# A hybrid retention, mixture-of-experts and attention kernel: where the expert weights are staged, and which engine works out the normalizations' factors

## What is computed

```python
x = x + retention(layernorm(x))   # 2 layers, 16 heads of 8, FFN 512, norms with gain and bias
x = x + moe(layernorm(x))         # 8 experts, the 2 best per token, silu(x w1) * (x w3) w2, F = 512
x = x + attention(layernorm(x))   # 16 heads of 8, causal softmax
x = x + moe(layernorm(x))         # the same weights
```

## Time and profile before

| | us |
|---|---|
| median of 3 runs (lowest, highest) | 889.42 (888.31, 891.47) |
| the profiled execution | 889.34 |
| its span | 887.3 |
| busy: TensorE, VectorE, ScalarE, GpSimd | 654.9, 609.1, 354.8, 294.6 |
| share of the chain that ended last: PE, DVE, "issue" | 55%, 16%, 10% |

### The profile page before, as it was taken

The page is one execution under the profiler, slowest core; times in us unless marked ns, Lnnn a source line. Parts: engine busy times, 40 slices in busy tenths (PEclk is TensorE's granted clock), DMA queues, the critical chain, the costliest instruction groups (busy, mean ns, idle before and its releaser), DMA issues.

```text
span 887.3 us, 19344 instructions
## 1 busy us (share of the span) xinstructions
PE 654.9 (74%) x6492; PEld 453.9 (51%) x6492; DVE 609.1 (69%) x1789; ACT 354.8 (40%) x605; POOL 294.6 (33%) x602
## 2 busy tenths in 40 slices
PE   2758998667868520999935788898898982499990
PEld 1434654435536420999933234444444442399990
DVE  2687876554686883688855677678678735387874
ACT  3204555453533420444414045555564561244440
POOL 1113344141433575355530201110512222355551
PEclk9788999987998855899976589999999995699995
DMA  9995211121100031556533512221312000265554
GB/s 229 193 184 120 96 49 48 48 66 31 49 19 2 3 81 46 146 165 171 167 120 101 130 30 56 76 57 46 101 40 67 15 14 18 81 171 152 167 146 148
DMA packets 102265, 81.00 MB, mean 91 GB/s; under 512 B 8380, under 2 KB 92412, under 8 KB 101980
## 3 DMA queue, kind: packets, MB, share of 16 engines
q1 hardware_dynamic: 96568, 68.35, 31.9%
q0 software_dynamic: 4544, 9.38, 3.1%
q10 hardware_dynamic: 1056, 2.04, 0.6%
HBM read 54.56 MB, written 23.20 MB: 88 GB/s over the span
## 4 chain that ended last, share of the span: by engine, by line
PE 55%; DVE 16%; issue 10%; DMA 6%; POOL 6%; ACT 4%; SPq 2%; ACTq 0%; DVEq 0%; POOLq 0%
PE PC L1999 8%; PE PA L1989 5%; PE PB L1989 5%; DVE rmax L1374 4%; POOL rows_dram L775 4%; PE PC L1905 4%; PE P L2077 4%; PE PA L2037 3%; PE PA L1883 3%; PE PA L2035 3%; PE P L1934 3%; PE P L1925 2%; PE P L1808 2%; DMA ffn_w<-in_w 2%; PE PC L2060 2%
## 5 line engine op out<-in xcount | busy, mean ns | idle before, releaser
L1374 DVE TENSOR_REDUCE rmax<-PA 128x1 f32<-128x512 f32 (+3 forms) x256 | 120.0, 489 | 50.1 <-PE PA L2037 43.3
L787 POOL DMA_INDIRECT outs_dram<-va,ids x78 | 81.2, 1041 | 94.4 <-DVE va L1313 89.9
L1999 PE MATMUL PC<-ffn_w,pm 128*128 128x128 f32 x624 | 87.0, 283 | 3.2 <-DMA ffn_w<-in_w 3.1
L775 POOL DMA_INDIRECT rows_dram<-va,idx x64 | 63.2, 988 | 77.9 <-DVE va L1242 59.1
L2037 PE MATMUL PA<-kst,qst 96*128 96x512 bf16 (+3 forms) x256 | 83.7, 332 | 0.0
L2035 PE MATMUL PA<-mqb,idb 128*128 128x128 bf16 x256 | 60.3, 237 | 24.7 <-DVE rmax L1374 17.4
L1999 PEld LDWEIGHTS PC<-ffn_w,pm 128*128 128x128 f32 x624 | 75.8, 192 | 4.6 <-DMA ffn_w<-in_w 3.9
L1641 ACT ACTIVATE kv_b<-P 128x256 f16<-128x256 f16 x78 | 29.9, 383 | 116.2 <-PE P L1978 116.2
L1303 DVE SCALAR_TENSOR_TENSOR pm<-PB,invb,decay 128x512 f32<-128x512 f32 x78 | 58.5, 750 | 19.5 <-ACT decay L1649 12.8
L2035 PEld LDWEIGHTS PA<-mqb,idb 128*128 128x128 bf16 x256 | 25.3, 99 | 86.9 <-DVE rmax L1374 47.6
L1989 PE MATMUL PA<-kv_b,pm 128*128 128x128 f16 x936 | 66.9, 223 | 0.0
(11 more groups left out here) (239 smaller groups left out, 1472.7 us busy)
## 6 DMA issues: line engine op xcount, KB each, us to landing
ffn_w<-in_w SPq DMA_DIRECT2D x78, 256.0 KB
rows_dram<-wall SPq DMA_DIRECT2D x1, 8385.0 KB, 54.0
X<-in_w SPq DMA_DIRECT2D x32, 256.0 KB, 2.9
proj_w<-rows_dram SPq DMA_DIRECT2D x78, 65.0 KB, 2.0
qst<-parts_dram SPq DMA_DIRECT2D x48, 96.0 KB
kst<-parts_dram SPq DMA_DIRECT2D x48, 96.0 KB
parts_dram<-qkp SPq DMA_DIRECT2D x16, 256.0 KB, 2.7
R<-outs_dram SPq DMA_DIRECT2D x4, 512.0 KB, 3.8
```

The source lines that it names most:

```text
L775: nc.gpsimd.indirect_dma_start(out=rows_dram, out_offset=bass.IndirectOffsetOnAxis(ap=idx[:, t, r:r + 1], axis=0), in_=xrow[:, t, :], in_o ...
L787: nc.gpsimd.indirect_dma_start(out=outs_dram, out_offset=bass.IndirectOffsetOnAxis(ap=ids[:, k % YB:k % YB + 1], axis=0), in_=ysb[:, k % Y ...
L1374: nc.vector.tensor_reduce(rmax[:, i, h % HG:h % HG + 1], PA[:, n % 2, 0:(i + 1) * P], AX_X, ALU.max).then_inc(pair_sb[n % 2], 1)
L1999: ins = mm(PC[:, k % 2, 0:D], eT[:, k % 2, f, :], w2b[k % WB2][:, f, :], start=f == 0, stop=f == FB - 1)
```

## The change

- **Weights.** Eight staging buffers, one per expert, are laid over the first buffers of `qst` and `kst`; each expert is loaded once, right behind the other inputs. In the place of the maximum of absolute values on VectorE comes the sum of absolute values on ScalarE (`weight_sum`, two in each of steps 4 to 7). The scales are made in step 9, high halves in steps 10 to 17, low halves in steps 12 to 19. The pad write follows the sums.
- **X.** x stays in X and is not loaded again. `add_shift` follows in step 3 of units 2 to 5.
- **Factors.** `mean_factors` on VectorE takes the place of GpSimd's `norm_factors` at 12 places: in step 1 of units 1 to 7, in step 0 of units 3 to 6, and for (LNM1, 0). `leave(0)` moves from step 30 to 29. ScalarE normalizes (LNM1, 0) a step earlier, and the router's first turn and product move ahead in TensorE's and ScalarE's streams.
- **Constant rows.** They are made by GpSimd after the blocks and filled by SyncE (four fills of 384 KB, then bo) behind the third w2 load of the first expert stage.
- Some buffers are doubled for this (`xrow_`, `parts_`, `below_`, `oneb_`, `cnt_`), by reuse of others.

```diff
+SUMS_AT, SCALE_AT, HIGH_AT, LOW_AT = 4, 9, 10, 12
-        stage = tuple(X[:, 8 * b:8 * b + 8, :].rearrange("p t n -> p (t n)") for b in range(2))
+        raw = tuple(stack[:, 0, :].bitcast(F32) for stack in (qst, kst))
+        stage = tuple(raw[2 * e // E][:, e % (E // 2) * 2 * F:(e % (E // 2) + 1) * 2 * F] for e in range(E))
+        all_sums = wall32[:, 0:2 * F]
...
@@ SyncE @@
-            sp.wait_ge(filled, 2)
-            for stack, fill in ((qst, zeros), (kst, ones)):
-                sp.dma_start(stack[KQ:KS, 0, :].rearrange("r (h n) -> r h n", h=H),
-                             fill.unsqueeze(1).to_broadcast([KS - KQ, H, L])).then_inc(stack_fill, 16)
...
+            for e in range(E):
+                sp.dma_start(stage[e][:, 0:F], a_w1[e]).then_inc(stage_in[e], 16)
+                sp.dma_start(stage[e][:, F:2 * F], a_w3[e]).then_inc(stage_in[e], 16)
...
                     w2_load(n, expert[n])
+                    if (m, n) == (0, 2):
+                        stack_constants()
+                        sp.dma_start(bo[:, :], a_bo.partition_broadcast(P)).then_inc(in_att, 16)
...
+            def stack_constants():
+                sp.wait_ge(filled, 3)
+                for b in range(2):
+                    for stack, fill in ((qst, zeros), (kst, ones)):
+                        sp.dma_start(stack[KQ:KS, b, :].rearrange("r (h n) -> r h n", h=H),
+                                     fill.unsqueeze(1).to_broadcast([KS - KQ, H, L])).then_inc(stack_fill, 16)
+            largest_weights()
             pad_rows()
-            for e in range(2 * E):
-                expert_in(e)
-                if e == E - 1:
-                    largest_weights()
             sp.wait_ge(w_hi, E)
             sp.wait_ge(w_lo, E)
-            for s in range(SEQ):
-                sp.dma_start(X[:, TPS * s:TPS * s + TPS, :], x_t[:, TPS * s:TPS * s + TPS, :]).then_inc(x_back[s], 16)
             sp.wait_ge(sc_ps, 2 * LAST)
-            sp.dma_start(kst[KQ:KS, 1, :], kst[KQ:KS, 0, :]).then_inc(stack_again, 16)
             sp.wait_ge(stats_sb, STAT[(LNM1, SEQ - 1)] + 1)
-            sp.dma_start(qst[KQ:KS, 1, :], qst[KQ:KS, 0, :]).then_inc(stack_again, 16)
...
@@ GpSimd @@
-                    if n == UNITS - 1:
-                        add_shift(0)
                 if u == 1:
-                    if SEQ <= n + 1 < UNITS:
-                        norm_factors(STAT[ln_in(n + 1)])
...
-                if u == 2 and n >= 1:
-                    norm_factors(STAT[ln_up(n - 1)])
-            norm_factors(STAT[(LNM1, 0)])
+                if u == 3 and 2 <= n < SEQ + 2:
+                    add_shift(n - 2)
             add_ffn2(UNITS - 2)
-            add_shift(1)
...
+            constant_rows()
             norm_factors(STAT[(LNM1, 1)])
             add_ffn2(UNITS - 1)
-            add_shift(2)
-            add_shift(3)
             norm_factors(STAT[(LNM1, 2)])
...
@@ VectorE @@
+                    if TPS < t < LAST and u == 1:
+                        mean_factors(STAT[ln_up(n - 1)])
                     if u == 0 and 3 <= n < SEQ + 3:
                         row_sums(R, n - 3)
                         means(*ln_in(n + 1))
+                        mean_factors(STAT[ln_in(n + 1)])
...
-                    if E - 1 <= t < 2 * E - 1:
-                        largest_weight(t - E + 1)
-                    if t == 2 * E + 1:
+                    if t == SCALE_AT:
                         weight_scales()
-                    if 2 * E + 2 <= t < 3 * E + 2:
-                        low_weight(t - 2 * E - 2)
-                    if t == LAST - 2:
+                    if LOW_AT <= t < LOW_AT + E:
+                        low_weight(t - LOW_AT)
+                    if t == LAST - 3:
                         leave(0)
+                        mean_factors(STAT[(LNM1, 0)])
...
@@ ScalarE @@
+            def weight_sum(e):
+                act.wait_ge(stage_in[e], 32)
+                if e >= 2:
+                    act.wait_ge(w_max, e - 1)
+                nc.scalar.activation(wall32[:, (1 + e % 2) * 2 * F:(2 + e % 2) * 2 * F], stage[e], ACT.Abs,
+                                     accum_out=amax[:, e:e + 1]).then_inc(w_max, 1)
...
                 act.wait_ge(w_scaled, 1)
-                act.wait_ge(stage_in[e % 2], 32 * ((E + e) // 2 + 1))
...
                 def weights(t):
-                    if 2 * E + 2 <= t < 3 * E + 2:
-                        high_weight(t - 2 * E - 2)
+                    if SUMS_AT <= t < SUMS_AT + E // 2:
+                        weight_sum(2 * (t - SUMS_AT))
+                        weight_sum(2 * (t - SUMS_AT) + 1)
+                    if HIGH_AT <= t < HIGH_AT + E:
+                        high_weight(t - HIGH_AT)
...
+                    if n == UNITS - 1:
+                        normalize(LNM1, 0)
...
@@ TensorE @@
+                    if t == LAST:
+                        plain_turn(LNM1, 0)
+                    if t == LAST + 1:
+                        router(0, 0).then_inc(ring_ps, 1)
...
-                route(0, 0)
                 down(UNITS - 2)
```

More of the change, by code:

```diff
@@ L175, in ring_plan @@
         if n >= 2:
-            plan += [("up", n - 2, f) for f in range(FB)]
+            plan += [("up", n - 2, 0), ("up", n - 2, 1)]
+        if n == UNITS:
+            plan += [("turn", LNM1, 0)]
+        if n >= 2:
+            plan += [("up", n - 2, 2), ("up", n - 2, 3)]
+        if n == UNITS:
+            plan += [("router", 0, 0)]
         if n + 1 < UNITS:
             plan += front(n + 1)
-        if n == UNITS:
-            plan += route(0, 0)
         if n == UNITS + 1:
@@ L338, in mixer_kernel @@
         state = sb("state", [P, 2, D])
-        below = state[:, 0, 0:P // 2].bitcast(BF16)
-        oneb = state[:, 0, P // 2:P].bitcast(BF16)
+        xrow_ = (xrow0, xrow1)
+        parts_ = [x[:, :, 0:D].bitcast(F16).rearrange("p t (i n) -> p t i n", i=2) for x in xrow_]
+        below_ = [x[:, 0:P // 2].bitcast(BF16) for x in (bo, state[:, 0, :])]
+        oneb_ = [x[:, P // 2:P].bitcast(BF16) for x in (bo, state[:, 0, :])]
         idh = state[:, 1, 0:P // 2].bitcast(F16)
@@ L353, in mixer_kernel @@
         lge = sb("lge", [P, 2, TPS, E])
-        scratch = (late[:, 0:2 * TPS * E * E], R[:, 2 * TPS:3 * TPS, :].rearrange("p k n -> p (k n)"))
+        scratch = tuple(R[:, c * TPS:(c + 1) * TPS, :].rearrange("p k n -> p (k n)") for c in (0, 2))
         cgt_, cge_ = ([x[:, i * TPS * E * E:(i + 1) * TPS * E * E].rearrange("p (k a b) -> p k a b", k=TPS, a=E)
@@ L415, in mixer_kernel @@
         in_att = sem("in_att")
-        stage_in = (sem("stage_ina"), sem("stage_inb"))
+        stage_in = [sem(f"stage_in{e}") for e in range(E)]
         w_max = sem("w_max")
@@ L607, in largest_weights @@
                 sp.wait_ge(amax_out, 16)
[L608 removed]
+                sp.dma_start(all_sums.rearrange("p (r e) -> p r e", e=E),
                              amax_dram.partition_broadcast(P)).then_inc(amax_in, 16)
@@ L1621, in blocks @@
                         gelu(n - 2, 3)
+                    if n == UNITS:
+                        keep_logits(0, 0).then_inc(freed("router", 0, 0), 1)
                     weights(TPS * n + 1)
@@ L1837, in count @@
                 pe.wait_ge(routed, c + 1)
+                pe.wait_ge(att_const, 1)
                 w = TPS * E
-                mm(bank[:, 0:w], below, taken[:, c % 2, :], start=True, stop=False, skip_group_check=True)
+                mm(bank[:, 0:w], below_[m], taken[:, c % 2, :], start=True, stop=False, skip_group_check=True)
                 for k in range(1, TPS):
-                    mm(bank[:, k * E:w], oneb, taken[:, c % 2, 0:w - k * E], start=False, stop=k == TPS - 1,
+                    mm(bank[:, k * E:w], oneb_[m], taken[:, c % 2, 0:w - k * E], start=False, stop=k == TPS - 1,
                        skip_group_check=True)
                 for k in range(TPS):
-                    ins = mm(bank[:, w:w + E], oneb, taken[:, c % 2, k * E:(k + 1) * E], start=k == 0,
+                    ins = mm(bank[:, w:w + E], oneb_[m], taken[:, c % 2, k * E:(k + 1) * E], start=k == 0,
                              stop=k == TPS - 1, skip_group_check=True)
```

89 lines of the change are left out of this document (37 added, 52 removed).

## The result

The changed kernel takes 893.88 us (890.69 to 896.59, 13 runs) where the kernel before takes 889.67 (887.63 to 893.95, 13 runs): a ratio of 1.0045, 95% interval 1.0027 to 1.0064. It is slower by 0.4%; the forecast was 881.2 and the range for all cases ended at 893. The profiled execution took 890.71 us with a span of 888.8, at the lower end of its runs.

What follows compares the result with a forecast made beforehand. TensorE was taken to bound units 2 and 3, a ring of waits through VectorE, ScalarE and TensorE to cost units 4 to 6 their excess. Terms summed to -8.2, giving 881.1 us; 869 to 893 held 8 in 10.

Steps and rivals of the forecast that it cites:

- the one on the constant rows: Expert tiles: SyncE's five issues take 5 to 10 us before the fourth w2 load; 3.5 us lost, bounds 0 and 8.
- The sum of the blocks: Start, units 2 to 6 and the blocks' end taken together: 10.2 us gained.
- Low halves: Steps 12 to 19: the wait before L973 disappears, leaving 1.2 us of VectorE per step, which is free.
- Chains: Factor chains on VectorE, 2.25 us each: 1.6 us lost in units 5 and 6; 4.0 with low halves in 3 and 4.
- Step 9: Unit 2: chain and scales make 5.2 us on VectorE; 4.2 us lost with half a clock drop.
- Step 5: A stretch bound by VectorE's own normalizations, so the chain costs its 2.25 us.
- step 29: Blocks' end: leave(0) moves here with a second chain behind it; 4.2 us more.
- The sums on ScalarE: Start: two Abs passes in step 6 put 2.4 us on the path, 0.85 for clock drops; table loads taken as 0.
- Shifts: Near 295 us: GpSimd's shifts move away, two VectorE delays of 1.0 us go, 0.5 may return; 1.5 us gained.
- Pad write: Behind the sums: issued at 91 us, landing at 145, before ScalarE's wait in step 17 at about 152.
- The signs: No wait before L973, units 5 and 6 under 28 us, TensorE waits of 2 us in units 3 and 4.
- The rivals: Chains absorbed (870, 17%); VectorE bounds first two steps (905 or 893, 15%); VectorE, GpSimd hinder (892, 6%); pad late (889, 5%).

Runs made afterwards that it cites:

- E5: Changed kernel with three of the four fills issued before the first expert stage, the fourth and bo behind its last w2 load: 882.85 us, ratio 0.9888.
- E8: The changed kernel run again unaltered, on another chip: 895.44 us, ratio 1.0037.
- E10: Changed kernel with its four fills issued by GpSimd behind its first scatter of results instead of by SyncE: 895.31 us, ratio 1.0066.
- E1: Changed kernel with the four fills and bo issued behind the last w2 load of the first expert stage, not the third: 889.19 us, ratio 0.9984.
- E2: Changed kernel with one fill each behind the w2 loads of tiles 2, 4, 6 and 8, bo behind tile 10: 888.74 us, ratio 0.9984.
- E7: Changed kernel with three fills before the first expert stage, all twelve factor chains on GpSimd and leave(0) in step 30: 864.51 us, ratio 0.9687.
- E3: Kernel before, with only each low half on VectorE moved one step after its high half on ScalarE: 867.67 us, ratio 0.9750.
- E9: Changed kernel with its four fills issued by ScalarE behind the first tile's silu instead of by SyncE: 895.18 us, ratio 1.0064.

## Why the prediction was wrong

**The step that failed** is the one on the constant rows: "so five issues are 5 to 10 us [...] I allow 3.5 us, bounds 0 and 8". The issues took 8.7 us, inside the 5 to 10. What failed is the overlap: I let only 3.5 us of them reach TensorE, and had no row for the slack that was to hide the rest. The term measured 11.2 us in the profiled execution, outside its bounds, and 12.6 by the medians of E5 and E8.

Hardly anything was hidden, because the fourth w2 load is never far ahead: its buffer comes free only when the first tile is done. In E5 it is issued at 355.66, lands by the median 3.0 us later and is used at 360.44, so the slack is some 1.8 us. In the changed kernel it is issued 11.7 us behind the third and not 1.8, thus 9.9 us late, and it takes 4.4 us to land (363.95 to 368.35). 9.9 + 1.4 - 1.8 = 9.5 us, and the wait is 9.60. Behind the wait the granted clock is 0.50 (365 to 370 us), the product takes 2.08 us for 1.11, and the next stands 3.9 us behind it and not 2.4. That is the rest of the 11.2.

There is a second cost, which I had not priced at all: time of the sixteen DMA engines, by E5 some 8.4 us of all of them, in a stretch where the w2 and row loads keep them at 0.57 to 0.68. The lines of the kernel before, then those of the changed one:

```profile
360.00:365.00 5.00, 4.38 (x60) 4.19 (x59) 3.96 (x10) 1.76 (x3) 1.26 (x2) 1.00 0.68 187
365.00:370.00 5.00, 5.00 (x75) 4.98 (x73) 4.23 (x11) 2.21 (x5) 2.92 (x5) 1.00 0.57 160
```

```profile
360.00:365.00 5.00, 0.00 (x0) 0.00 (x0) 0.70 (x2) 0.00 (x0) 0.13 (x1) 0.62 0.78 157
365.00:370.00 5.00, 1.65 (x7) 1.66 (x8) 0.00 (x0) 0.00 (x0) 0.00 (x0) 0.50 0.70 185
```

In the changed kernel the engines stand at 0.78 and 0.70 during the wait, so on the average of all sixteen they are not full, and the late issue is what TensorE waits for. In E10 SyncE is free of the fills, the share is 1.04, and the cost is there all the same. So E10 rules out that the queue's order alone makes the cost; with the late issue taken away, full engines stand in its place. Whether less than all sixteen engines limit the fills is not shown. E1 and E2 show that lateness or spreading recovers about half, and E5 shows that the place decides: before the expert stage the DMA share was 0.14 to 0.25, SyncE had nothing else to issue, and nothing is lost.

**The sum of the blocks** was nearly right, -8.3 for -10.2, but two terms inside covered each other's errors.
- *Low halves*: "1.2 us in a step are free". They are not: by E7 a unit with the weight work takes 29.1 and 28.8 us and one without 25.9, at a clock of 0.94 instead of 1.00 (E3: 29.1 and 28.8 with it). In the changed kernel it is 30.4 and 30.5 for 27.1. The two halves cost 3 us a unit, not nothing.
- *Chains*: in units 3 and 4 I charged 4.0 us and half a clock drop, 4.9 in all; they cost 1.3 and 1.7. In units 5 and 6 it was 1.2 and 1.1 for 1.6. A unit without anything is 25.9 and not 25.0, so the units came to 27.1 for a forecast of 26.6. That the totals of all four are near the forecast is luck.
- *Step 9*: its chain cost 3.9 us (E7 has the scales there too, and its unit 2 takes 26.29 for 25.00 before), chain and scales together 5.2 for 4.2. *Step 5* cost 2.2 (2.25), *step 29* 4.4 (4.2).
- *The sums on ScalarE*: the start without its chain is 85.63 us (E7), so they cost 2.1 for a forecast of 2.4 and 0.85 of clock. The pair in step 6 takes 2.08, in the timeline of the changed kernel's ScalarE, ahead of the normalization of the earlier trace rows:

```profile
79.45 1.08 ACT L1579 ACTIVATE wall<-kst 128x1024 f32<-128x1024 f32 x1
...
80.49 1.08 ACT L1579 ACTIVATE wall<-kst 128x1024 f32<-128x1024 f32 x1
...
81.53 1.65 ACT L1596 ACTIVATE xn<-R,nrm 128x128 f32<-128x128 f32 x4
```

  No table load stands before them, so the 0 to 2.6 us were 0, and the Trainium skill (ScalarE: Activation LUTs, "Table sets: the hidden batching unit"), by which every set has abs, agrees with the trace.
- *Shifts*: -2.0 for -1.5. The kernel before had three such delays, not the two I counted (1.19 to 1.20 us at 294.16, 295.38 and 296.61); one is left, 1.19 us at L883 at 285.88, beside GpSimd's bias sum of 1.26 us.
- *Pad write*: it was issued at 88.64 and landed 51.9 us later, at 140.5 (forecast 91 and 145); ScalarE never waited.

**The median** lay another 2.7 us above the before's than the profiled pair shows (4.2 for 1.5): the profiled execution of the changed kernel lay at the lower end of its runs (890.71 in 890.69 to 896.59), and E8's, at 895.64, is the same up to 351 us and later in the expert stages and the attention. What makes those longer from one execution to the next stays open.

**The signs.** As forecast, VectorE has no wait before the low halves, units 5 and 6 are under 28 us at full clock, and TensorE waits 2.4 us in units 3 and 4. In units 5 and 6 it waits 1.30 and 1.02 us, for none over 1. The wait before the fourth tile's product is 9.6 us, for 2 to 6.

**The rivals.** None of the four came in. VectorE did not become the bound: the chains took 15.8 us and were charged some 24 with their clock drops (2.25 + 4.2 + 9.8 + 3.2 + 4.2). Of VectorE and GpSimd hindering each other nothing shows in the twelve chains: each takes 2.16 to 2.18 us from its first start to its last. The change ended on the slow side through the term that I held for small.

**The change in two halves**, which I should have priced apart: the weight part without the fills' burst is worth 26.4 us (E7), the burst costs 12.6 to 15.1, the chains 15.8 by the traces and 16.8 by medians of different chips (893.9 less 877.1) or 18.3 by those of one chip (882.9 less 864.5, E5 and E7). The weight part's gain is little more than that of E3's single step, 26.4 for 23.0.

## What to carry to other kernels

Price a transfer that goes into a busy stretch twice: by its issue, against the slack of the next load in that queue, and by the DMA engines' time it takes, against the share left over there. Here the late issue was the limit in one kernel and the full engines in another, at much the same cost, so another queue didn't help and an idle stretch did. Where a ring of waits holds three engines, try first to move one member a step later: that alone gave 23 us here, with everything else kept. Two halves of a change that share no wait are to be priced, and run, one by one, since a gain of 26 us can hide behind two losses that together are larger.

## What the runs showed that I had not expected

- The fills look like poor work for the DMA engines. Beside them (24 partitions of 16 KB each) all sixteen stood at 1.04 for 109 to 128 GB/s (E10), where the expert loads alone move 154 to 171 GB/s at 0.58 to 0.59 (E5, 355 to 365 us).
- Issues get longer behind other fills: the first fill took SyncE 1.03 us at 352.65, the fourth 2.31 at 356.81, and ScalarE 1.45 and 2.31 in E9. It is not the expert loads that do it: in E5, in a stretch without them, the third fill took 2.22 us (315.92). GpSimd issued its four in 0.68 to 0.81 us each (E10).
- VectorE hinders GpSimd too. In E7 an operation of four columns in GpSimd's chain, whose others there take about 0.20 us, took 1.23 while VectorE made a low half (120.45 to 121.72):

```profile
120.55 1.23 POOL L719 TENSOR_TENSOR nrm<-nrm 128x4 f32<-128x4 f32 x1
```

- A chain on GpSimd takes 5.1 us (302.54 to 307.60 in the kernel before), over twice VectorE's 2.25, and the stage was 15.8 us shorter with all twelve there (E7): what counts is what stands behind the chain in its engine's stream.
